# Delta-rule phase: the loop over head groups as a loop of the chip, and projections ahead of the norm sums

## The reference, cut to what matters

```
qkv = x @ w_qkv ; z = x @ w_z ; beta, g from x @ w_b, x @ w_a
conv = silu(causal_conv(qkv, 4 taps));  q, k, v = split(conv)
core = chunk_gated_delta_rule(q, k, v, g, beta)     # per head: decays, a triangular solve, a mix with q k^T
out  = core * rsqrt(mean(core * core) + EPS) * norm_w
out  = out * silu(z)
x    = x + out @ w_out
```

## Time and profile before

| | |
|---|---|
| median of 3 runs | 1736.31 us (1731.66 to 1739.67) |
| profiled execution, its own time | 1736.31 us |
| its span | 1734.1 us |
| PE busy | 1477.6 us (85%), 8504 matmuls |
| DVE busy | 1101.2 us (64%) |
| ACT busy | 825.2 us (48%) |
| POOL busy | 372.0 us (21%) |
| delta phase, first to last load of `wz` | 184.4 to 1076.1 us, 7 groups |

### The profile page before, as it was taken

How to read it: one execution, slowest core, us unless ns; L and a number is a source line. 1 busy time by engine, 2 the same in 40 slices (tenths; PEclk the granted TensorE clock), 3 DMA queues, 4 the chain that set the end, 5 groups by cost and what they waited for, 6 DMA issues and landing times. The chain is left out here.

```text
span 1734.1 us, 22906 instructions
## 1 busy us (share of the span) xinstructions
PE 1477.6 (85%) x8504; PEld 845.7 (49%) x8504; DVE 1101.2 (64%) x1984; ACT 825.2 (48%) x1688; POOL 372.0 (21%) x321
## 2 busy tenths in 40 slices
PE   0126789999999989999989989989789999798998
PEld 0112447557547547557547547547434444344333
DVE  6996584784784784794784793772477878613112
ACT  3033476676676676676676675676111111211111
POOL 7101001302202201301301301304123333200222
PEclk9978889999999999999999999989899999998999
DMA  1001000000000000000000000000201111200010
GB/s 60 0 0 52 37 14 13 25 14 13 25 13 14 25 14 13 25 14 13 25 14 13 25 13 13 1 13 1 84 30 45 45 43 41 75 0 26 26 38 37
DMA packets 15644, 43.02 MB, mean 25 GB/s; under 512 B 3618, under 2 KB 6842, under 8 KB 14394
## 3 DMA queue, kind: packets, MB, share of 16 engines
q1 hardware_dynamic: 15546, 41.69, 7.0%
HBM read 39.58 MB, written 2.10 MB: 24 GB/s over the span
## 5 line engine op out<-in xcount | busy, mean ns | idle before, releaser
L956 DVE SCALAR_TENSOR_TENSOR conv<-bank,taps,conv 128x510 f32<-128x510 f32 (+2 forms) x384 | 282.9, 744 | 85.6 <-ACT conv L745 76.6
L449 PE MATMUL bank<-rT,wf 128*128 128x512 f32 x512 | 253.5, 629 | 41.0 <-DMA wf<-in_wf_dram 33.2
L1356 ACT ACTIVATE ffn_relu<-bank 128x512 f32<-128x512 f32 x100 | 59.7, 597 | 300.8 <-PE bank L1495 300.8
L1514 PE MATMUL bank<-ffn_weighted,ffn_chunk 128*128 128x512 f32 x400 | 192.2, 604 | 2.0 <-DVE ffn_weighted L1473 2.0
L1495 PE MATMUL bank<-rT,ffn_chunk 128*128 128x512 f32 x400 | 192.9, 607 | 0.0
L449 PEld LDWEIGHTS bank<-rT,wf 128*128 128x128 f32 x512 | 98.1, 200 | 153.0 <-issue 137.2
L1327 POOL TENSOR_TENSOR ffn_relu<-ffn_relu 128x512 f32<-128x512 f32 x96 | 107.2, 1116 | 247.9 <-ACT ffn_relu L1356 247.9
L1473 DVE TENSOR_TENSOR ffn_weighted<-ffn_relu,bank 128x512 f32<-128x512 f32 x96 | 65.9, 688 | 147.5 <-POOL ffn_relu L1327 136.4
L745 ACT ACTIVATE conv<-bank,taps 128x512 f32<-128x512 f32 x128 | 88.9, 715 | 134.3 <-PE bank L449 134.3
L1082 POOL TENSOR_TENSOR sq<-sq,qsq 128x512 f32<-128x512 f32 x64 | 81.3, 1271 | 292.4 <-ACT sq L901 290.7
L1103 POOL COPY pT<-sq 32x1024 f32<-32x1024 f32 x32 | 33.1, 1035 | 483.3 <-DVE sq L1042 481.9
(11 more groups left out here) (254 smaller groups left out, 2776.6 us busy)
## 6 DMA issues: line engine op xcount, KB each, us to landing
ffn_chunk<-in_L_chunks_dram SPq DMA_DIRECT2D x25, 512.0 KB
wf<-in_wf_dram SPq DMA_DIRECT2D x8, 1024.0 KB, 4.8
wz<-in_wz_dram SPq DMA_DIRECT2D x8, 512.0 KB, 3.2
wo<-in_wo_dram SPq DMA_DIRECT2D x8, 512.0 KB, 3.4
ffn_spread<-in_L_spread_dram SPq DMA_DIRECT2D x33, 40.0 KB
side<-in_fT_dram SPq DMA_DIRECT2D x1, 1024.0 KB, 5.0
xT<-in_xT_dram SPq DMA_DIRECT2D x1, 1024.0 KB, 8.9
gate_dram<-gate SPq DMA_DIRECT2D x1, 1024.0 KB, 3.9
```

The source lines that it names most:

```text
L449: last = pe.matmul(banks[b][:], wf[:, c, n // NH, :], rT[:, c, halves(n % NH)], start=(c == 0), stop=(c == CT - 1))
L956: dve.scalar_tensor_tensor(acc[:, :, k:], src[:, :, 0:T - k], taps[:, n // NH, KS - 1 - k:KS - k], acc[:, :, k:], ALU.mult, ALU.add).then_inc(
L1514: last = pe.matmul(banks[4 + 2 * c + h][:], chunk[:, slot, CT + t, c * P:(c + 1) * P], hw[:, u, :], start=start, stop=stop, skip_group_che ...
```

## The change

The helper `groups` calls group 0, then opens a loop of the chip over groups 1 to 6, and then calls group 7. POOL, which has no special last group, loops over 1 to 7. Group number and semaphore values are then registers inside the loop.

In the mixing stage the order changes on three engines. PE does `project_v(n)` right behind `mix(n)`, and `rms(n - 2)` after it; `k_norm(0)` comes behind `project_v(1)`, `k_norm(1)` ahead of `project_v(3)`. ACT does `take_tap(HF + n)` ahead of `root(n - 2)`. DVE does `convolve` ahead of `normalize(n - 2)`, and both `normalize(6)` and `normalize(7)` fall into the next group.

```diff
     def groups(eng, group):
-        for g in range(NG):
-            group(g, g == 0, g == NG - 1)
+        group(0, True, False)
+        with eng.Fori(1, NG - 1) as g:
+            group(g, False, False)
+        group(NG - 1, False, True)
...
                 mix(g, n)
+                if not last_group:
+                    if n == 3:
+                        pe.wait_ge(conv_ready, p * NF * NH + 6)
+                        k_norm(p, 1)
+                    project_v(p, n)
+                    if n == 1:
+                        pe.wait_ge(conv_ready, p * NF * NH + 5)
+                        k_norm(p, 0)
                 if n >= 2:
...
                     rms(g, n - 2)
-                if not last_group and n >= 1:
-                    project_v(p, n - 1)
-                    if n < 3:
-                        pe.wait_ge(conv_ready, p * NF * NH + 4 + n)
-                        k_norm(p, n - 1)
-            pe.wait_ge(ln_done, g * NU + NU - 3)
-            rms(g, NU - 2)
-            if not last_group:
-                project_v(p, NU - 1)
-            pe.wait_ge(ln_done, g * NU + NU - 2)
-            rms(g, NU - 1)
+            for n in (NU - 2, NU - 1):
+                pe.wait_ge(ln_done, g * NU + n - 1)
+                rms(g, n)
...
-                if n >= 2:
-                    root(g, first, n - 2)
-                if n >= 1:
-                    take_tap(HF + n - 1)
+                take_tap(HF + n)
...
+                if n >= 2:
+                    root(g, first, n - 2)
             root(g, first, NU - 2)
-            take_tap(HF + NU - 1)
             root(g, first, NU - 1)
...
             if not first:
+                normalize(g - 1, 6)
                 normalize(g - 1, 7)
...
-                if n >= 1:
-                    normalize(g, n - 1)
                 fill(HF + n)
+                if n >= 2:
+                    normalize(g, n - 2)
...
-        for g in range(NG):
-            group(g, g == 0)
+        group(0, True)
+        with pool.Fori(1, NG) as g:
+            group(g, False)
```

More of the change, by code:

```diff
@@ L1068, in vector @@
         groups(dve, group)
-        normalize(NG - 1, 7)
+        for n in (6, 7):
+            normalize(NG - 1, n)
         for u, b in enumerate((4, 5, 6, 7)):
```

## The result

The changed kernel has a median of 1759.44 us in 4 runs (1756.61 to 1766.88), beside 1737.99 us for the kernel before in 4 runs on the same chip (1731.66 to 1743.74): a ratio of 1.0131, with a 95% interval of 1.0083 to 1.0179. It is slower, by 1.3%. The forecast was 1749, the range 1722 to 1768. The profiled execution took 1759.95 us, its span 1758.1.

What follows compares the result with a forecast made beforehand. PE was taken to set the pace of the delta phase, with 8.5 idle us in a group. The terms gave 1736.3 - 14 + 3 + 15 + 8.5 = 1748.8, so 1749 us, range 1722 to 1768.

Steps and rivals of the forecast that it cites:

- The new order: Seven borders between groups: three PE waits go, a smaller one comes, 2.0 us gained each; -14 us (0 to -21).
- Registers: Loop body: added register instructions cost 0.5 us an iteration where a blocked engine must compute; +3 us (0 to +12).
- The branch back: Loop's end, five times: PE refetches the loop's code, 2.95 us a border; +15 us (0 to +18).
- the price of one refill: PE's branch back to code that isn't there: 3.7 us from when PE's sequencer takes the branch.
- The clock: Behind PE's idle time at the branch: 3.4 us at half speed lose 1.7 us, five times; +8.5 us (0 to +25).
- DVE and ACT hidden behind PE: Loop's head: delays from DVE's and ACT's own branches stay behind PE's delay; without it DVE's would cost 1.4 us.
- The rival in which the body stays near PE: Loop's code isn't fetched again, so no PE stall and the clock stays: 1725 to 1730 us; chance 0.20.
- the dry spots: Solve: PE runs out of instructions, 2.8 and 3.4 us in two groups; if gone, up to 15 us less.
- The rival of DVE's circle: Mixing stage: tap, convolution and scaling on DVE come late, a step exceeds 3.88 us, gain lost: 1763 us; chance 0.13.
- the gap without releaser: Groups 2 to 6: PE idles some 3 us ahead of `gram(0)` with no other engine answering; not in groups 1 and 7.
- the vanished waits: Mixing stage: the two PE waits of 0.84 us at `rms`, for ACT's Ln of `k_norm`, are gone.
- POOL's wait: Border: PE has one wait of about 1 us ahead of the last `rms`, released by POOL.

Runs made afterwards that it cites:

- e1: Changed kernel with the new order but every group written out, no loop on any engine: 1717.12 us, ratio 0.9887 to the kernel before.
- e10: Changed kernel with the hinted back edge, plus 83 idle products on PE ahead of the first projection: 1711.30 us, ratio 0.9854 to the kernel before.
- e8: Changed kernel with the compiler's hint for the loop's back edge on each engine but POOL: 1728.50 us, ratio 0.9947 to the kernel before.
- e7: Changed kernel with SP's 1-MB load of `wf` held back until the group's fourth Gram product: 1753.58 us, ratio 1.0093 to the kernel before.
- e6: Changed kernel with five idle products on PE behind the last `rms` in the loop's groups: 1751.06 us, ratio 1.0073 to the kernel before.
- e3: Changed kernel with the loop on PE only, all other engines written out: 1759.87 us, ratio 1.0123 to the kernel before.
- e4: Changed kernel with PE's groups written out, the loop kept on all other engines: 1734.14 us, ratio 0.9980 to the kernel before.
- e11: Changed kernel with the hinted back edge, plus 40 idle products on PE ahead of the first projection: 1706.35 us, ratio 0.9821 to the kernel before.
- e2: Kernel before with the loop over groups on every engine as in the changed kernel, old order kept: 1768.55 us, ratio 1.0168 to the kernel before.

## Why the prediction came out as it did

The time fell in the range and in the direction that had the largest chance, and the mechanism named was the one at work. The size was 10 us short: 1759.4 lies 2 us above the forecast's own range of 1741 to 1757, and only the room kept for the rivals covers it. The terms missed in both directions, so that the sum came this near is in part luck. Measured in the same units, against the kernel before:

- **The new order**, -14 predicted, -19.8 measured (e1). The border gained 2.23 us where I took 2.0. I had not counted the 6.1 us from the solves; in a kernel whose stalls depend on where 256-instruction packets end, that part belongs to the layout of the code as much as to the order, and I can't separate the two.
- **Registers**, +3 predicted, none seen. In e10 all registers are there, and a solve takes 33.1 to 33.3 us in groups 2 to 6, as in the best groups of e1 (33.4, 33.1); a border without a stall takes 38.7 us in e8 with registers and 38.8 in e1 without, a middle 54.2 in both. The inversion's steps, where I had looked for them, are in the changed kernel what they were in the earlier trace rows:

```profile
L1034 DVE TENSOR_TENSOR rs<-rs,tmp 128x31 f32<-128x31 f32 (+15 forms) x248 | 85.0, 343 | 7.8
```

- **The branch back**, +15 predicted, 5 x 4.14 = +20.7 measured. The term that was too small is the price of one refill, 3.70 us from the earlier trace rows, where PE's branches took 4.8 to 5.5: at the place of those rows no load was under way (DMA share 0.02 from 641 to 645 us). The second pair of those rows, 4.52 us apart, is none, as its 1.11 us is the wait for ACT named above; the sum did not use it. With the load moved (e7) the same distance is 2.83 us where I had worked out 2.95. The loads of `wf`, `wz` and `wo` I had only asked whether they come in time, not what they do to the refill.
- **The clock**, +8.5 predicted, 5 x 2.32 = +11.6 measured, confirmed by e6 (11.3). I had taken 3.4 us at the low level; it was 6.8 four times and 3.4 once.
- **DVE and ACT hidden behind PE**: right for the changed kernel (e3, 1759.87, equals it). Their price without PE's delay, which I put at 1.4 us a border, is 3.1 us (e4).
- **Not in the sum: the solve inside the loop**, +9.9 against e1. It goes away where the body stays in the store (e10), so it belongs to the refills. In the six solves PE is idle without a releaser for 12.6 us, in e1 for 8.0 besides the wait for ACT, and busy 4.0 us longer, at the lower clock. That a loop body has its page's ends at the same place in every pass fits this, but how much of it is the layout alone the runs do not separate.

These add to 1737 - 19.8 + 20.7 + 11.6 + 9.9 = 1759.4. A gain that was too small by 5.8 and a cost for registers that does not exist stood against 18.7 us of cost not counted.

The rival in which the body stays near PE had a chance of 0.20 and a time of 1725 to 1730, 1712 if the dry spots go too. In the changed kernel it is wrong. The runs show that the same body can be brought to stay, by the hint and 80 instructions of offset, at 1706 us. The rival of DVE's circle was not seen: no `mix` waits for `normalize` in the steady part. Of the signs that I had named, the gap without releaser, the vanished waits, POOL's wait and the clock came; the packets did not stay at 60 to 70 (78), and the windows were 131.7 to 136.2 us where I had said 131 to 134.

Of the two sections of the Trainium skill that the prediction set against each other, the one on "Instruction fetch mechanics" ("Runtime: NRT & Kernel Launch") describes the changed kernel: a branch back out of its window stalls for a fetch, 4.8 to 5.5 us in the trace. The one on "ISA Cache" ("Advanced Engine Details and Errata") gives 128 KB for TensorE in lines of 16 KB; that agrees with e11, where some 1,968 instructions pass five times without a packet. Each of the two sections also speaks of two lines or pages alone, and with that e11 does not agree. What decides between the two cases here is the hint.

## What to carry to other kernels

- A loop in the place of written-out code costs, on each engine, the refetch at the branch back. It counts only where the engine has nothing queued ahead of the branch: look at the last instruction of the body. If it waits for another engine, the refetch is bare, and a drop of the clock may follow.
- A change that removes a wait can take away the cover of another cost. The order and the loop were worth -19.8 and +31.6 us alone; together +21.5, not +11.8. In the old order PE's refetch was covered, and ACT's (5.0 us a border in e2) was what PE waited for; the new order laid PE's bare, 6.5 us, and hid ACT's behind it.
- Look for instruction packets inside the loop first. If they are there, try the hinted back edge, and then a shift of the code: here the two took 53 us off the same loop, and the shift without the hint nothing.

## What the runs showed of the hardware that I had not expected

- The hinted branch back takes PE 0.42 to 0.49 us in e8 in the place of 3.3 to 5.5. The queue that refills the other engines (q14) then has no packet between 384 and 1154 us, where without the hint it had 10 of 8 KB in every pass, for 333 instructions on VectorE and 281 on ScalarE. So a branch back without the hint refetches code that was in the store; why, the runs do not show.
- A shift of 80 instructions changed PE from 9 refill packets in each pass to none, and the kernel from 1728.50 to 1706.35 us, most of it by that. A body of 1,967 instructions fits into eight packets from 81 or 82 of 256 starting places (2,048 less its length, and one), and the shifts of 80 and 166 lie 86 apart. That both do is not explained, and no other shift was run.
- PE's sequencer was 3.6 us ahead of its array in e2 (451.46 to 455.07) and took a branch of 3.3 us without a gap.
